# State space layer: B and C go as rows to DRAM and come back broadcast by DMA, C then copied to one of two PSUM banks; another order of the first pass

## The reference, cut to what matters

```
xn     = layernorm(x)
xi, z  = split(xn @ W_in.T)                      # 512 and 512 channels
u      = silu(causal_conv4(xi, W_conv) + b_conv)
for each direction d (forward, backward):
    dt, B, C = split(u @ Wx_d.T, [64, 16, 16])   # B, C: 16 states per time step
    delta    = softplus(dt @ Wdt_d.T + bdt_d)
    h[t]     = exp(delta[t] * A) * h[t-1] + delta[t] * u[t] * B[t]
    y_d[t]   = sum over states of h[t] * C[t]  +  D_d * u[t]
x      = x + ((y_f + y_b) / 2 * silu(z)) @ W_out.T
```

## Time and profile before

| | |
|---|---|
| Median of 3 runs | 4832.25 us (4831.99 to 4836.26) |
| Profiled execution | 4826.13 us, span 4824.3 us |
| Granted TensorE clock, mean | 0.918 |
| PE, DVE, ACT, POOL busy in the span | 85%, 66%, 45%, 28% |
| DMA | 45.79 MB in 9176 packets |

### The profile page before, as it was taken

The page is one execution under the profiler, slowest core; times in us unless marked ns, Lnnn a source line. Parts: engine busy times, 40 slices in busy tenths (PEclk is TensorE's granted clock), DMA queues, the critical chain, the costliest instruction groups (busy, mean ns, idle before and its releaser), DMA issues.

```text
span 4824.3 us, 59405 instructions
## 1 busy us (share of the span) xinstructions
PE 4088.0 (85%) x21276; PEld 2776.0 (58%) x21276; DVE 3205.9 (66%) x7409; ACT 2179.8 (45%) x5294; POOL 1353.9 (28%) x876
## 2 busy tenths in 40 slices
PE   5677877867799996999899998788798779778989
PEld 2222323323466775998788886455565558436767
DVE  3878888888765665666688896566576654534751
ACT  3554655646444441222233336467676532423331
POOL 2776767678300000000122223364220000100011
PEclk8888988989999997999999999789899989878999
DMA  1000000000000000000000000000000000000000
GB/s 48 0 0 0 0 0 0 1 0 0 37 1 1 1 1 38 27 18 10 12 1 1 1 1 37 12 1 1 11 2 2 1 36 1 36 0 18 1 1 18
DMA packets 9176, 45.79 MB, mean 9 GB/s; under 512 B 715, under 2 KB 5939, under 8 KB 6451
## 3 DMA queue, kind: packets, MB, share of 16 engines
q1 hardware_dynamic: 8883, 42.00, 2.4%
HBM read 39.90 MB, written 2.10 MB: 9 GB/s over the span
## 4 chain that ended last, share of the span: by engine, by line
PE 33%; DVE 12%; ACT 4%; issue 2%; POOL 1%; DMA 0%; DVEq 0%; ACTq 0%; POOLq 0%
PE PS L208 27%; PE PS L215 4%; DVE qg L1885 1%; ACT p L2363 1%; DVE stat L285 1%; PE PS L2867 1%; DVE p L3146 1%; DVE qg L1880 1%; DVE XNr L322 1%; ACT p L3159 1%; DVE sm L1396 1%; DVE wc L3071 0%; DVE p L2594 0%; DVE p L3311 0%; DVE sm L2592 0%
## 5 line engine op out<-in xcount | busy, mean ns | idle before, releaser
L1018 DVE TENSOR_TENSOR_SCAN db<-PS,db 128x512 f32<-128x512 f32 x512 | 593.0, 1205 | 81.5 <-ACT PS L986 46.4
L208 PE MATMUL PS<-db,cst 128*128 128x512 f32 x1024 | 520.3, 647 | 0.0
L215 PE MATMUL PS<-cst,p 128*128 128x128 f32 (+1 forms) x2880 | 398.2, 285 | 54.2 <-DVE pt L2831 23.6
L1701 POOL TENSOR_TENSOR rb<-rb,tb 128x512 f32<-128x512 f32 x32 | 41.2, 1287 | 1341.4 <-DVE tb L1696 1341.4
L208 PE MATMUL PS<-part,selb 96*128 96x512 bf16 x512 | 179.8, 410 | 270.2 <-DVE db L1025 191.6
L215 PEld LDWEIGHTS PS<-cst,p 128*128 128x128 f32 (+1 forms) x2880 | 339.3, 150 | 106.3 <-issue 38.0
L208 PE MATMUL PS<-xnT,W 128*128 128x256 f32 (+1 forms) x1184 | 381.6, 470 | 21.2 <-ACT pt L2389 8.8
L966 POOL TENSOR_TENSOR db<-W,b 128x1024 f32<-128x1024 f32 x128 | 311.6, 2445 | 153.1 <-PE PS L208 67.9
L966 POOL TENSOR_TENSOR db<-du,b 128x1024 f32<-128x1024 f32 x128 | 302.3, 2374 | 135.4 <-PE PS L208 80.7
L208 PEld LDWEIGHTS PS<-db,cst 128*128 128x128 f32 x1024 | 215.0, 210 | 208.7 <-issue 193.3
L208 PEld LDWEIGHTS PS<-xnT,W 128*128 128x128 f32 x1184 | 232.0, 200 | 160.4 <-issue 114.6
(11 more groups left out here) (423 smaller groups left out, 9056.5 us busy)
## 6 DMA issues: line engine op xcount, KB each, us to landing
W<-in_we SPq DMA_DIRECT2D x9, 1024.0 KB, 4.8
W<-in_w SPq DMA_DIRECT2D x1, 4224.0 KB, 13.0
W<-in_w SPq DMA_DIRECT2D x1, 4122.5 KB, 14.8
W<-in_w SPq DMA_DIRECT2D x1, 4100.0 KB, 12.0
W<-in_w SPq DMA_DIRECT2D x1, 2770.0 KB, 15.5
W<-in_w SPq DMA_DIRECT2D x1, 2313.0 KB, 9.3
X<-in_x SPq DMA_DIRECT2D x4, 512.0 KB, 5.8
W<-in_w SPq DMA_DIRECT2D x1, 2048.0 KB, 8.0
```

The costliest lines, as they stand in the source:

```text
L208: ins = T.matmul(out, l, r, start=first and i == 0, stop=last and i == len(pairs) - 1)
L215: ins = T.transpose(bank[0:m, c:c + r], s, ident[0:r, 0:r])
L1018: V.tensor_tensor_scan(db[:, f, r], self.ring.PS[:, self.BANKS[x % 3], r], db[:, f, r], 0.0, ALU.mult, ALU.add).then_inc(self.sc.sem, 1)
```

## The change

B and C are no longer split, selected and broadcast by PE. The projection `Wxd` gives dt, B and C in one 96-row result; ACT copies it to `dtb`; SP writes the 32 rows of B and C to a DRAM tensor (`sp_piece`), and for every unit loads row s of B and of C back into SBUF tiles with a partition broadcast (`sp_b`, `sp_c`; 128 x 512 fp32, three tiles each). POOL reads both from SBUF. For the units whose product with C is DVE's, ACT copies C from SBUF to one of two PSUM banks, between its two exponentials (`act_c`, called in `act_da`). db has six buffers instead of five, and the ring has three banks instead of four. ABS becomes a piece of its own, and the addition of a layer output to x (ADDX) comes one step after its matmul.

In the first pass the first quarter of x, Win and the context are loaded first, x is normalized before the context, blocks 2 and 3 of the convolution are made on DVE, and softplus and delta * u are done in two halves, the subtraction on DVE.

```diff
 class Start
     def sp(self, e):
         for c in range(4):
             (load quarter c of x)
-        if self.context:
-            (load the context)
-        E.load_weights(e, LAYERS[0])
+            if c == 0 and self.first:
+                e.eng.dma_start(E.region(0)[:, 0:2048], A["w0"][:, 0:2048]).then_inc(self.win.sem, 16)
+            if c == 0 and self.context:
+                e.eng.dma_start(self.raw[0:S2], A["ctx"].rearrange("b s d -> s b d")).then_inc(self.ctx_in.sem, 16)
+            if c == 0:
+                E.load_weights(e, LAYERS[0], 2048 if self.first else 0)
     def dve / act / pe:
+        for s in range(32):
+            self.nxt.dve(e, s, self.nxt.early)
         if self.context:
             self.dve_context(e)
-        for s in range(32):
-            self.nxt.dve(e, s, self.nxt.early)
 class Mamba
-    CBANK = 4
+    CBANKS = (3, 4)
-        self.db = [E.tile(f"db{i}", 1024) for i in range(5)]
-        self.c_ = [E.tile(f"c{i}", 512) for i in range(2)]
-        self.b_ = [E.tile(f"b{i}", 512) for i in range(2)]
+        self.db = [E.tile(f"db{i}", 1024) for i in range(6)]
+        self.c_ = [E.tile(f"c{i}", 512) for i in range(3)]
+        self.b_ = [E.tile(f"b{i}", 512) for i in range(3)]
+        self.bc = E.nc.dram_tensor("bc_rows", (8, 32, 512), F32, kind="Internal").ap()
-        one = {self.DT: 0, self.DT + 1: 1, self.DTA: 2, self.BC: 7, self.BC + 1: 8, self.EXP: 8, self.BCA: 9,
-               self.LN: 9, self.MAX: 10, self.PART: 10, self.SUB: 11, self.PART + 1: 11, self.ADD: 12, self.DU: 13}
+        one = {self.DT: 0, self.DT + 1: 1, self.DTA: 2, self.ROWS: 5, self.ABS: 8, self.EXP: 9, self.LN: 10,
+               self.MAX: 11, self.SUB: 12, self.ADD: 13, self.DU: 14}
+    FIRST = (2, 30, 3, 31, 8, 10, 0, 28, 1, 29, 4, 5, 32, 6, 7, 33, 12, 13, 14, 15, 27, 16, 36, 17, 37, 18, 38, 19, 39,
+             ABS, EXP, LN, MAX, SUB, ADD, DU)
     def sp(self, e):
+        self.steps(e, self.nothing, self.nothing, self.sp_piece, self.sp_b, self.sp_c, self.nothing)
         (the end of the layer, then the next weights)
+    def sp_piece(self, e, what, k, j):
+        if what == self.READY and j == self.ROWS:
+            e.wait_ge(*self.dta(k + 1))
+            e.eng.dma_start(self.bc[k], self.dtb[64:96, :]).then_inc(self.rows.sem, 16)
+    def sp_b(self, e, i):
+        e.wait_ge(*self.rows(k + 1))
+        e.wait_ge(*self.gb(i - 2))
+        e.eng.dma_start(self.b_[i % 3], self.bc[k, s].partition_broadcast(P)).then_inc(self.bd[i % 3].sem, 16)
+    def sp_c(self, e, i):
+        e.wait_ge(*self.c_used(i - 3))
+        e.eng.dma_start(self.c_[i % 3], self.bc[k, 16 + s].partition_broadcast(P)).then_inc(self.cd_[i % 3].sem, 16)
     def dve_piece: (PART, PART + 1 removed)
+        if j == self.MAX:
+            for r, x in self.halves(k):
+                (t2 = max(delta, 0) + t2;  delta = (t1 + 1) - 1)
+                if k == 0:
+                    (t1 = t1 - delta;  delta = t2 + t1, both on DVE)
+        elif self.CONV <= j < self.SILU and k == 0 and j % 2 == 0 and j >= self.CONV + 4:
+            (block f = 2, 3: u = x0 * w0 + b, then three u = xi * wi + u)
-    def pe_b(self, e, i):
-    def act_b(self, e, i):
     def pool_b(self, e, i):
-        e.wait_ge(*self.ab(i + 1))
-        e.wait_ge(*self.du_(k + 1))
-        e.wait_ge(*self.sum_of(i - 5))
+        e.wait_ge(*self.bd_(i))
+        e.wait_ge(*self.du_(k + 1, p if k == 0 else 1))
+        e.wait_ge(*self.sum_of(i - 6))
     def act_da(self, e, i):
         for f in range(2):
             (the exponential)
+            if f == 0 and not self.on_pool(i):
+                self.act_c(e, i)
     def act_c(self, e, i):
-        if i < self.NU and self.on_pool(i):
-            x = self.pools(i)
-            e.wait_ge(*self.pc(i + 1))
-            e.wait_ge(*self.cm(x - 1))
-            e.eng.activation(self.c_[x % 2], self.ring.PS[:, self.CBANK, :], ACT.Copy).then_inc(self.ca.sem, 1)
+        e.wait_ge(*self.cd_of(i))
+        e.wait_ge(*self.h(i - self.pools(i) - 1))
+        e.eng.activation(self.cbank(i), self.c_[i % 3], ACT.Copy).then_inc(self.ca.sem, 1)
     def pe_tail(self, e, i):
-        if i < self.NU:
-            c, p, d, k, s = self.of(i)
-            if i:
-                e.wait_ge(*(self.ca(self.pools(i)) if self.on_pool(i - 1) else self.made(i - 1)))
-            bank = self.ring.PS[:, self.CBANK, :]
-            mm(T, bank, [(self.sel_c[0:96, 16 + s, :], self.part[d][0:96, :])]).then_inc(self.pc.sem, 1)
         for j in self.sums(i):
             (the sums, as before)
```

More of the change, by code:

```diff
@@ L507, in pe @@
     def pe(self, e):
+        for s in range(32):
+            self.nxt.pe(e, s, self.nxt.early)
         if self.context:
             self.pe_context(e)
-        for s in range(32):
-            self.nxt.pe(e, s, self.nxt.early)
     def pe_context(self, e):
@@ L734, in pe @@
         self.enter(e)
[L735 to L738, removed]
+        self.mine = self.ring.without(self.CBANKS + self.BANKS)
+        self.steps(e, self.inn.pe, self.nxt.pe, self.pe_piece, self.nothing, self.nothing, self.pe_tail)
         for t in range(12, 16):
@@ L788, in pe_piece @@
                 self.pe_out(e, 4 * k + j)
+        elif what == self.ADDX:
+            return
         elif what == self.GATE:
@@ L797, in pe_piece @@
             self.inn.wait(e, c)
-            e.wait_ge(*self.w_ready)
-            bank = ring.take(e, ("win", c, f), self.upa(4 * c + f + 1))
+            e.wait_ge(*self.E.win_ready)
+            bank = ring.take(e, ("win", c, f), self.upa(self.nth_win(c, f)))
             mm(T, bank, [(self.Win[:, i, f * P:(f + 1) * P], self.E.xnT[:, i, c * 512:(c + 1) * 512])
@@ L811, in pe_piece @@
                 ins.then_inc(self.cv.sem, 1)
-                ring.release(("conv", c, f), self.ua(4 * c + f + 1))
+                ring.release(("conv", c, f), self.ua(4 * c + f - 1 if c else f + 1))
         elif self.DT <= j < self.DTA:
             half, wd = j - self.DT, v4(W[f"Wxd{d}"])
+            e.wait_ge(*self.w_ready)
             e.wait_ge(*self.silu(c + 1))
             bank = ring.of(("dt", k)) if half else ring.hold(e, ("dt", k))
-            ins = mm(T, bank[0:64, :], [(wd[:, i, :], v4(self.u)[:, i, :]) for i in (2 * half, 2 * half + 1)],
+            ins = mm(T, bank[0:96, :], [(wd[:, i, :], v4(self.u)[:, i, :]) for i in (2 * half, 2 * half + 1)],
                      half == 0, half == 1)
@@ L886, in act_piece @@
                          bias=W[f"bdt{d}"][:, f:f + 1]).then_inc(self.dla.sem, 1)
+        elif j == self.ABS:
+            e.wait_ge(*self.dla(4 * k + 4))
+            for r, x in self.halves(k):
+                C.activation(v4(self.t1)[:, r, :], v4(delta)[:, r, :], ACT.Abs).then_inc(e.own, e.up())
         elif j == self.EXP:
-            e.wait_ge(*self.dla(4 * k + 4))
-            C.activation(self.t1, delta, ACT.Abs).then_inc(e.own, e.up())
             e.wait_ge(e.own, e.ups)
[L891 to L895, removed]
+            for r, x in self.halves(k):
+                t = v4(self.t1)[:, r, :]
+                C.activation(t, t, ACT.Exp, scale=-1.0).then_inc(self.ee.sem, 1)
         elif j == self.LN:
             e.wait_ge(*self.E.z_ready)
-            e.wait_ge(*self.ee(k + 1))
-            C.activation(self.t2, self.t1, ACT.Ln, bias=self.E.one).then_inc(self.ln.sem, 1)
+            for r, x in self.halves(k):
+                e.wait_ge(*self.ee(x))
+                C.activation(v4(self.t2)[:, r, :], v4(self.t1)[:, r, :], ACT.Ln,
+                             bias=self.E.one).then_inc(self.ln.sem, 1)
     def dve_piece(self, e, what, k, j):
         V = e.eng
-        if what == self.OUT and j:
-            self.dve_to_x(e, 4 * k + j - 1)
+        if what == self.ADDX and j < 4:
+            self.dve_to_x(e, 4 * k + j)
         if what != self.READY:
@@ L1060, in pe_sum @@
         for f in range(2):
-            ins = mm(T, self.ring.of(("y", g, f)), [(self.E.ident, split(self.db[i % 5], 2)[:, f, :])], first=False,
+            ins = mm(T, self.ring.of(("y", g, f)), [(self.E.ident, split(self.db[i % 6], 2)[:, f, :])], first=False,
                      last=d == 1 and s == 15)
```

228 lines of the change are left out of this document (126 added, 102 removed).

## The result

The changed kernel takes 4640.2 us (median of 4 runs, 4636.61 to 4641.53) against 4832.12; the ratio is 0.9600, 95% interval 0.9583 to 0.9617: 192 us faster. The profiled execution took 4640.26, its span is 4638.1. The prediction was 4655, range 4585 to 4790.

A forecast was written before the change was run, and what follows sets the result against it. DVE was taken as nearest the bound, starved through PE's and ACT's queues, with DVE and POOL's balance as floor. Gains of 151 us in the loop and 24 in the first pass gave about 4655 us, range 4585 to 4790.

The forecast's parts named there:

- The loop's sum: First layer's loop: 902 us of DVE work plus 118 idle gives 1020 us, a gain of 151.
- DVE's idle time: DVE in the first layer's loop after the change: 118 us in all, bounds 60 and 160.
- the small ones: DVE's minor waits in the loop (normalization copies, table waits): some 30 us before, 25 after.
- POOL's long pieces: 14 POOL operations of 4.5 us in the loop; its lead covers half, leaving DVE 31 us of waiting.
- The landing: Time for a 256 KB broadcast of B or C to arrive: 3.2 us, ends 2.8 and 4.7.
- the circle: SP's in-order loop of two issues, one transfer's arrival and two POOL products: 8.8 us, under the pace of 9.4.
- rival B: Broadcasts in the loop arrive too late, at 4.7 us: some 64 us lost, 4719 to 4780 in all; chance 17%.
- PE's one ring bank: One bank left for PE's pieces, so PE waits at each; costed at nothing in the loop, six db buffers covering it.
- The first pass: Start of the kernel up to the first scan: 24 us saved, bounds 15 and 30, first scan near 69 us.
- the halves save what the first half needn't wait for: Between Abs and the first scan: softplus and delta * u in halves save about 10 of 27.2 us.
- C: Rival: 128 reads of one DRAM row are slow; at 51 GB/s the loop takes 2630 us, total about 6290; chance 15%.
- D: Rival: PE falls behind by over six buffers at pieces, POOL waits for sums; 4740 us in all; chance 6%.

## Why the prediction was right

**The direction and the cause.** The slow stretches of the earlier trace rows were read as PE's queue standing at pieces and banks with B in it. The runs bear it out: B's way alone is worth 77 us of loop, C's 37, the split 61, together nearly the distance from 1170.8 to 991.9. These runs take away the work together with its place in the queues; that the place is what costs is read from the waits, and from PE's being busy only 74% of the loop, and no run separates the two.

**The loop's sum**, 151 predicted and 170 measured, is two errors that half cancel. *DVE's busy time* was set at 902 us and is 922: I took away the split and left all else as it was. The row of the normalization before (L322 there) is

```profile
L322 DVE TENSOR_SCALAR XNr<-X,stat 128x256 f32<-128x256 f32 x24 | 16.3, 739 | 0.2
```

and it grew from 16.3 to 34.3 us for the same 24 operations. The transfers are not the reason: in the kernel without B and C, which moves 3 GB/s over its loop, these operations take 1.63 us. POOL is busy 73% of the loop before, 86% in the changed kernel and 88% in that one, so I take it that DVE's operations with both ends in SBUF meet POOL's more often; no run shows this by itself. *DVE's idle time* was set at 118 us and is 80: the wait for POOL was sized at 45 us and is 11.3 for B and 12.8 for the subtraction; ACT's was sized at 32 and is 17.4, the gate's 16 and is 12.6; the small ones, sized at 25, are what is left, 25.5. My 31 us for POOL's long pieces supposed a lead of 2.3 us in front of each of the 14; the waits show five stalls before a scan and four before the sum.

**ACT's copy of C**, taken at 0.58 us and nothing on the path: it takes 0.58 to 0.60, and ACT's busy time is 594 where 575 was the estimate; where the other 20 us come from is open.

**The landing**, taken at 3.2 us, is 3.6, so the circle is 0.9 + 3.6 + 4.7 = 9.2 us against a pace of 9.4. Its direction is right, its price is not. With the third transfer it has three issues and landings of 5.3 us for b, 1.3 + 5.3 + 4.7 = 11.3 us; at 80 triples that would be some 150 us, and the loop is 66 us longer. That the 66 come near the 64 of rival B is luck, since the 64 were worked out for a circle of 10.3. Two things were wrong in it. The pace of 9.4 us was read at the loop's end, where no pieces stand: over the whole changed loop three units take 11.7 us. In its quickest stretches they take 10.0 us (60 scans in 100 us), and 10.9 with the third transfer (55 scans), so the circle can bind there and not in the slow stretches. And the delay reaches DVE through ACT's wait for C, not through POOL's wait for B. The estimate of 2.6 us for 256 KB from the Trainium skill (DMA: Bandwidth & Descriptors, "Anatomy of one DMA") is 1.0 us below what landed here with another transfer in flight; by that figure the third one would have been free, and it was not.

**PE's one ring bank** costs nothing that can be seen: POOL's 4.6 us. No run gave the ring its fourth bank back, or took the sixth db buffer away.

**The first pass**, 24 us predicted and 18.3 measured. Win starts at 21.13 (21.5 predicted) and Abs at 51.56 (52). These rows of the timeline show what follows:

```profile
51.56 2.00 ACT L956 ACTIVATE tt<-W 128x1024 f32<-128x1024 f32 x2
...
63.99 3.19 POOL L1027 TENSOR_TENSOR W<-W 128x1024 f32<-128x1024 f32 x1 [63.15 <-DVE W L988]
...
70.33 2.34 POOL L1027 TENSOR_TENSOR W<-W 128x1024 f32<-128x1024 f32 x1 [3.15 <-DVE W L988]
72.62 9.26 POOL L1035 TENSOR_TENSOR db<-W,b 128x1024 f32<-128x1024 f32 x4
75.00 2.34 DVE L1089 TENSOR_TENSOR_SCAN db<-PS,db 128x512 f32<-128x512 f32 x2 [4.75 <-POOL db L1035]
```

From Abs to the first scan it is 23.4 us, 3.7 less than before where I had 10. The step that failed is "the halves save what the first half needn't wait for": POOL's program has both halves of delta * u ahead of its first unit, so the first unit waits for the second half whatever the semaphores say. In the rows POOL ends the first half at 67.2 us, waits 3.15 us for DVE's second half and works 2.34 on it, 5.4 of the missing 6.3 us. That all units may as well wait for both halves, without any difference, agrees; POOL's order itself was not changed in any run.

**The rivals.** B did not happen with two transfers per unit; with three its landings and POOL's waits come, though the loss takes another path. C falls by the 191 GB/s of one-row broadcasts; why the mask moved at 50 GB/s no run shows. D falls by the short waits for PE's sums.

## What to carry to other kernels

When two engines with in-order queues carry an operand to a third, the time lost can lie less in the copies than in what stands in those queues, as the waits say here: count who is behind whom before counting microseconds, and look at the pace by stretches. A queue that has nothing else to do (here SP with its DMAs) can carry it nearly for free as long as the circle of release, issue, landing and use stays under the pace. Work that circle out by stretches, and for every engine that waits for the transfer: here the loop lost 66 us when landings came 1.7 us later, and the wait that reached the bound engine was that of ACT, which has a copy between two exponentials, not the one that I had watched. And look where an operand lies: in PSUM the product ran at 1.22 us beside POOL, in SBUF at 2.38.

## What the runs showed of the hardware

- Broadcasts of one 2 KB row of DRAM to 128 partitions land in 3.6 to 3.7 us with two per unit of 3.9 us, and their 137 GB/s is no ceiling: 191 GB/s over the loop with three.
- A third transfer of a quarter of the bytes raised the landings of b from 3.6 to 4.8 us, one of the full size to 5.3. Most of the delay came with a quarter of the bytes; that it is the number of packets is likely, but not shown.
- A DVE product with both inputs in SBUF took twice as long beside a busy POOL (2.38 against 1.22 us), and POOL's products with B took a fifth longer (2.99 against 2.44 us), all of it shown as busy time.
- DVE's normalization, with one tile in SBUF as input and one as output, took 0.41 us before the loop and 1.49 in it; in a loop without the broadcasts it took 1.63, so they don't cause it.
- The granted TensorE clock over the loop stayed as it was (0.88 before, 0.87 after) although PE has 134 us less to do in it.
